# Self-attention with one score product: the maximum is subtracted by VectorE and the probabilities are transposed

## The reference

```python
scores = jnp.einsum('bhqd,bhkd->bhqk', q, k) * scale          # scale = 1/4
scores = jnp.where(causal[None, None], -jnp.inf, scores)      # mla and attn only
attn = jax.nn.softmax(scores, axis=-1)
out = jnp.einsum('bhqk,bhkd->bhqd', attn, v)
```

## Time and profile before

| what | value |
|---|---|
| median of 3 runs | 1013.06 us (1012.3 to 1020.51) |
| the profiled execution | 1020.58 us |
| its span, first to last instruction | 1018.5 us |
| PE, DVE, ACT busy | 971.9, 608.3, 450.8 us |
| TensorE clock granted, mean | 0.973 of full speed |

### The profile page before, as it was taken

One profiled execution on the slowest core, in us unless ns is written; L12 is line 12 of the kernel. 1 busy time (PEld: TensorE's weight loads), 2 busy tenths in 40 slices (PEclk: granted clock), 3 DMA queues, 4 the chain that ended last, 5 costly groups with the idle time before them and its releaser, 6 DMA issues.

```text
span 1018.5 us, 25940 instructions
## 1 busy us (share of the span) xinstructions
PE 971.9 (95%) x10769; PEld 832.1 (82%) x10769; DVE 608.3 (60%) x1427; ACT 450.8 (44%) x899; POOL 167.5 (16%) x357
## 2 busy tenths in 40 slices
PE   5999999999999989999879999997999999999998
PEld 5888888888888877788659999995888887877887
DVE  5745644554332646577579787777777763464242
ACT  3333333333333356655216666661444534574241
POOL 2312212113112113233330000003211200111000
PEclk9999999999999979999779999998999999999999
DMA  9400000000000092000028999964231002000000
GB/s 319 137 10 22 1 23 21 1 2 1 2 1 1 20 362 113 2 13 13 22 63 270 363 364 358 357 178 88 43 55 33 13 3 70 6 3 1 1 21 22
DMA packets 93763, 86.46 MB, mean 85 GB/s; under 512 B 42632, under 2 KB 85072, under 8 KB 93136
## 3 DMA queue, kind: packets, MB, share of 16 engines
q1 hardware_dynamic: 92112, 80.62, 24.8%
q0 software_dynamic: 1536, 4.20, 1.3%
HBM read 75.62 MB, written 9.18 MB: 83 GB/s over the span
## 4 chain that ended last, share of the span: by engine, by line
PE 86%; DVE 7%; ACT 4%; issue 2%; DMA 0%; POOL 0%; DVEq 0%; ACTq 0%; POOLq 0%
PE ps L632 9%; PE ps L647 9%; PE ps L2327 7%; PE ps L2340 6%; PE ps L2663 6%; PE ps L616 3%; PE ps L664 3%; PE ps L1446 3%; PE ps L1155 3%; PE ps L586 3%; PE ps L1543 3%; PE ps L684 3%; PE ps L1485 2%; PE ps L1080 2%; PE ps L1090 2%; PE ps L1527 2%
## 5 line engine op out<-in xcount | busy, mean ns | idle before, releaser
L2327 PE MATMUL ps<-moe_xT,ew 128*128 128x128 f32 x736 | 92.1, 280 | 2.2 <-issue 1.3
L775 ACT ACTIVATE x0pT<-ps 128x512 f32<-128x512 f32 x64 | 38.3, 598 | 123.6 <-PE ps L647 123.6
L2327 PEld LDWEIGHTS ps<-moe_xT,ew 128*128 128x128 f32 x736 | 88.4, 196 | 3.3 <-DVE moe_xT L2413 1.9
L385 POOL TENSOR_TENSOR rn_tmp<-rn_cur,eps 128x1 f32<-128x1 f32 x48 | 13.1, 273 | 354.0 <-DVE rn_cur L379 353.8
L890 DVE TENSOR_TENSOR x0A_lo<-ps,x0A_hi 128x512 fp32r<-128x512 f32 x64 | 41.1, 685 | 31.8 <-ACT x0A_hi L766 31.7
L2663 PE MATMUL ps<-f,ffw 128*128 128x512 f32 x256 | 59.1, 391 | 0.8 <-issue 0.6
L2663 PEld LDWEIGHTS ps<-f,ffw 128*128 128x128 f32 x256 | 47.7, 188 | 11.5 <-issue 0.9
L2340 PE MATMUL ps<-ew_2hi,eh_hi 128*128 128x256 f32 x184 | 55.4, 301 | 0.9 <-DVE eh_lo L2466 0.5
L2276 DVE TENSOR_TENSOR ew_2lo<-ew,ew_2hi 128x1024 fp32r<-128x1024 f32 x46 | 55.9, 1216 | 0.0
L2523 POOL DMA_INDIRECT yg<-moe_out,slot x16 | 16.1, 1006 | 232.3 <-DMA moe_out<-moe_y 163.5
L632 PE MATMUL ps<-x0wv_hi,x0cT_hi 128*128 128x512 f32 x128 | 52.8, 413 | 0.6 <-DVE x0A_lo L890 0.6
(11 more groups left out here) (332 smaller groups left out, 2459.9 us busy)
## 6 DMA issues: line engine op xcount, KB each, us to landing
ew<-L_ffn_W_dram SPq DMA_DIRECT2D x46, 1024.0 KB, 7.7
x0cin<-ctx_dram SPq DMA_DIRECT2D x8, 512.0 KB, 3.9
x1cin<-ctx_dram SPq DMA_DIRECT2D x64, 64.0 KB, 2.3
moe_out<-moe_y SPq DMA_DIRECT2D x23, 128.0 KB, 4.1
xg<-moe_in SPq DMA_DIRECT2D x21, 128.0 KB, 7.7
moe_in<-padneg SPq DMA_DIRECT2D x2, 1024.0 KB, 12.6
maskrow<-mask_BxS_ik_dram SPq DMA_DIRECT2D x2, 1024.0 KB, 7.6
x0wk<-L_xattn_Wkv_dram SPq DMA_DIRECT2D x1, 1024.0 KB, 7.1
```

The source lines that it names most:

```text
L775: nc.scalar.activation(g.pT[:, u, :], ps[:, S_BANK[u % 2], :], ACT.Exp, scale=64.0 ** -0.5).then_inc(C0.exp, 1)
L2327: last = nc.tensor.matmul(ps[:, n % 3, j * BT:j * BT + BT], ew1[b % NW][:, i, f * P:f * P + P], xT[b % 2][:, i, :], start=(i == 0), stop=( ...
```

## The change

The second score product goes away, with the negative maxima, their transposition, their tables and copies. After the maximum, DVE subtracts it from the scores in PSUM and writes the difference (128x1024, float32) to SBUF, into one of two tiles `sa_P` that lie in the memory of `xw`. ACT takes the exponential in place, one iteration earlier than before (item n+1 in iteration n). PE transposes the probabilities, eight 128x128 tiles in two ring fills "P0" and "P1" after `fill_pv` of n-1; ACT empties the first into the lower half of `sa_pT` (`pT_lower`), DVE the second into the upper half (`pT_upper`). The copy of k moves from DVE to ACT, that of v from ACT to DVE. The router's product comes after `fill_v`, and `fill_T` before it. Since `sa_P` uses its memory, `xw` is loaded later, at block 9 of the experts, with its axes exchanged. `keep_clock` issues 3, 4 and 3 matmuls where it issued 3, 2 and 2, and 2. The list `_more` says which fills DVE empties.

The diff, cut to its core:

```diff
+        sa_P = [nc.alloc_sbuf_tensor_at(f"sa_P{i}", [P, 4, D], F32, offset=xw_at + 16 * D * i) for i in range(2)]
...
-                FILLS += _routed(_n - 3, "router") + _at(_n + 2, "v") + _at(_n + 3, "hT") * _early + _at(_n - 1, "T", "y")
+                FILLS += _at(_n, "P0", "P1") + _at(_n - 1, "T") + _at(_n + 2, "v") + _routed(_n - 3, "router") + _at(_n + 3, "hT") * _early + _at(_n - 1, "y")
...
-        _more = [(n, "v") for n, (k, _) in enumerate(ITEMS) if k == "mla"] + [(n, k) for n, k in FILLS if k[0] == "A"]
+        _more = [(n, k) for n in range(3 * T) for k in ("v", "P1")] + [(n, k) for n, k in FILLS if k[0] == "A"]
...
             def scores(n):
...
-                if n > lo + 1:
-                    pe.wait_ge(SA.exp, n - 1)
-                elif n > lo:
-                    pe.wait_ge(SA.max, n)
+                if n > lo:
+                    pe.wait_ge(SA.shift, n)
...
-            def fill_neg(n):
...
-            def exponents(n):
...
+            def fill_P(n, half):
+
+                if half == 0:
+                    pe.wait_ge(SA.exp, n + 1)
+                RS.wait_free(pe, n, f"P{half}")
+                for i in range(4):
+                    r, hf = 2 * half + i // 2, i % 2
+                    last = nc.tensor.transpose(RS.bank(n, f"P{half}")[:, i * P:i * P + P], sa_P[n % 2][:, r, hf * P:hf * P + P], ident)
+                last.then_inc(SA.fill, 1)
 
             def fill_pv(n):
 
-                pe.wait_ge(SA.exp, n + 1)
+                RS.wait_emptied(pe, n, "P0")
+                RS.wait_emptied(pe, n, "P1")
...
             def exps(n):
-                act.wait_ge(SA.e_ps, n + 1)
-                nc.scalar.activation(g.pT[:, :, :], QS[:, :, 0:D], ACT.Exp, scale=0.25).then_inc(SA.exp, 1)
+                act.wait_ge(SA.shift, n + 1)
+                nc.scalar.activation(sa_P[n % 2][:, :, :], sa_P[n % 2][:, :, :], ACT.Exp, scale=0.25).then_inc(SA.exp, 1)
...
+                exps(lo)
...
             for n in range(lo, hi + (2, 1)[span]):
...
-                if here:
-                    exps(n)
+                if ahead:
+                    exps(n + 1)
...
             def maximum(n):
...
-                nc.vector.tensor_scalar(g.neg[:, :, 0:4], g.max[:, :, :], -1.0, None, ALU.mult).then_inc(SA.neg_hi, 1)
-                dve.wait_ge(SA.neg_hi, n + 1)
-                nc.vector.scalar_tensor_tensor(g.neg[:, :, 4:8], g.max[:, :, :], -1.0, g.neg[:, :, 0:4], ALU.mult, ALU.subtract).then_inc(SA.neg, 1)
...
+                nc.vector.tensor_tensor(sa_P[n % 2][:, :, :].rearrange("p r (f k) -> p r f k", f=4), QS[:, :, 0:D].rearrange("p r (f k) -> p r f k", f=4),
+                                        g.max[:, :, :].rearrange("p r (f o) -> p r f o", o=1).broadcast_to((P, 4, 4, N)), ALU.subtract).then_inc(SA.shift, 1)
...
-                elif front and (span == 0 or n > lo):
-                    k(n + 2)
                 if back:
                     attend(n - 1)
+                if here:
+                    pT_upper(n)
...
+                if front:
+                    v(n + 2)
...
-            for i, w in enumerate(("Wq", "Wk", "Wv", "Wo")):
-                whole(xw[:, :, i, :], weight("L1_xattn_" + w), ld["xw"])
...
+                if b == 9:
+                    RS.wait_filled(sp, 2 * T - 1, "P1")
+                    for i, w in enumerate(("Wq", "Wk", "Wv", "Wo")):
+                        whole(xw[:, i, :, :], weight("L1_xattn_" + w), ld["xw"])
```

More of the change, by code:

```diff
@@ L836, in self_tables @@
             dve.wait_ge(SA.tri, 1)
[L837 to L843, removed]
+            nc.vector.tensor_scalar(bqc_par[:, :], par_of, vec("bqc"), None, ALU.mult).then_inc(SA.tables, 2)
         def dve_x0(dve):
@@ L1171, in fill_y @@
                 for k in range(KD):
-                    last = nc.tensor.matmul(R1.bank(t, "y")[:, 0:D], g.attT[:, k, :], xw[:, k, 3, :], start=(k == 0), stop=(k == KD - 1))
+                    last = nc.tensor.matmul(R1.bank(t, "y")[:, 0:D], g.attT[:, k, :], xw[:, 3, k, :], start=(k == 0), stop=(k == KD - 1))
                 last.then_inc(C1.fill, 1)
@@ L1487, in scores @@
                 last.then_inc(SA.s_ps, 1)
-            def fill_neg(n):
-                pe.wait_ge(SA.neg, n + 1)
-                RS.wait_free(pe, n, "neg")
-                nc.tensor.transpose(RS.bank(n, "neg")[:, 0:N].bitcast(BF16), g.neg[:, :, :].rearrange("p r c -> p (r c)"), identb[:, :]).then_inc(SA.fill, 1)
-            def exponents(n):
[L1496 to L1512, removed]
-                                                    g.qbd[n % 3][32 * r:32 * r + 32, hf, b, :, :].rearrange("p a n -> p (a n)"),
-                                                    start=False, stop=True, skip_group_check=True)
-                last.then_inc(SA.e_ps, 1)
+            def fill_P(n, half):
[6 more added lines that the diff above has]
+                last.then_inc(SA.fill, 1)
             def fill_pv(n):
-                pe.wait_ge(SA.exp, n + 1)
+                RS.wait_emptied(pe, n, "P0")
+                RS.wait_emptied(pe, n, "P1")
                 pe.wait_ge(SA.v_frame, 3 * span + 3)
@@ L1692, in pe_self @@
                         fill_qk(n + 2, "q")
-                    if span == 0 and hi - 2 <= n <= hi:
-                        RS.wait_free(pe, n - 1, "T")
-                        keep_clock(RS.bank(n - 1, "T"), 3 if n == hi - 2 else 2)
                     if back:
@@ L1698, in pe_self @@
                 final = n - hi if span == 0 else None
-                if routed(span, n - 3):
-                    fill_router(n - 3)
+                if here:
+                    fill_P(n, 0)
+                    fill_P(n, 1)
                 if final == 1:
@@ L1704, in pe_self @@
                     place(5)
+                if final in (-2, -1, 0):
+                    RS.wait_free(pe, n - 1, "T")
+                    keep_clock(RS.bank(n - 1, "T"), 4 if final == -1 else 3)
+                if back:
+                    fill_T(n - 1)
                 if front:
                     fill_v(n + 2)
+                if routed(span, n - 3):
+                    fill_router(n - 3)
                 early = mla_pair(n + 2)
@@ L1824, in act_self @@
                 hT(lo)
+                k(lo)
                 x1_neg(t, 0)
@@ L1831, in act_self @@
                 x1_exps(t, 0)
+                k(lo + 1)
                 q(lo + 1)
-                v(lo + 1)
                 hT(lo + 2)
                 x1_exps(t, 1)
+                k(lo + 2)
                 x1_attT(t)
                 q(lo + 2)
+                exps(lo)
             for n in range(lo, hi + (2, 1)[span]):
-                here, front, back = lo <= n < hi, n + 2 < hi, lo <= n - 1 < hi
-                if here:
-                    neg(n)
+                here, ahead, front, back = lo <= n < hi, n + 1 < hi, n + 2 < hi, lo <= n - 1 < hi
                 if span == 1 and n > hi - 3:
                     f = 3 * (n - hi + 2)
-                    for i in range(f, min(f + 3, FT)):
-                        ff_relu(act, i)
-                if span == 1 and n == hi:
-                    ff_upper(act, 4)
-                    ff_upper(act, 5)
+                    ff_relu(act, f)
+                    if here:
+                        ff_relu(act, f + 1)
                 if is_mla(n + 2):
@@ L1880, in self_begin @@
         def self_begin(dve, span):
-            nc.vector.memset(SB.neg[:, :, :], 0.0).then_inc(SA.ready, 1)
+            dve.sem_inc(SA.ready, 1)
             if span == 1:
@@ L1988, in dve_self @@
             for n in range(lo, hi + (4, 1)[span]):
-                ahead, front, back = lo <= n + 1 < hi, n + 2 < hi, lo <= n - 1 < hi
+                here, ahead, front, back = lo <= n < hi, lo <= n + 1 < hi, n + 2 < hi, lo <= n - 1 < hi
                 if span == 1 and n == hi - 3:
```

141 lines of the change are left out of this document (72 added, 69 removed).

## The result

The changed kernel takes 1050.62 us (median of 4, 1047.35 to 1052.48) against 1016.78 for the kernel before in the same runs: a ratio of 1.0328, 95% interval 1.0261 to 1.0395. The forecast was 1035 against 1013.06, a ratio of 1.022. The direction and the mechanism came out. The size fell short: 33.8 us were lost and 22 forecast.

What follows compares the result with a forecast made beforehand. PE was taken as full, with DVE's queue setting when hT starts. Terms 7.0 + 2.0 + 3.3 + 2.6 - 2.0 + 1.0 = 13.9, with the clock 22, put on 1013.06: 1035 us; range 1006 to 1056, the forecast's own 1025 to 1047.

Steps and rivals of the forecast that it cites:

- Slot iterations: Iterations 9, 11, 13: hT starts 7.1 us after s, the start of probabilities times values; 2.35 lost each, +7.0 us.
- Iterations 10 and 12: Same walk with the shorter group for the top experts in place of the slots; 1.0 each, +2.0 us.
- Iterations 4, 6 and 8: An mla item is projected: transposed output 1.1 us later, the output projection waits for it; +3.3 us.
- Start: Iterations 0 to 3: ACT's queue carries two more table loads of 1.28 us each; +2.6 us.
- The clock: PE's waits in iterations 9, 11, 13 bring two or three further clock falls; +8 us, from 0 to 25.
- Experts and second cross-attention: Expert stage: 1 MB of weights loaded there is hidden behind expert weights; 2.9 us if that cover is gone.
- Iterations 5, 7 and the drain: Iterations 5 and 7, 14, 15 and the drain: late v costs 1.0 us in all, 0 to 2.
- The rival that PE's relief is kept: Late v and routing hidden, 17 us off, less table loads 14: 999; decided by h ready by about s+3.8; chance 0.12.
- span 1: Only 0.2 of PE's 0.86 us relief left, five times; first and last items another 1: -2.0, between 0 and -6.9.
- rule on weight loads: Weight loads, 6.91 of 8.89 us, would leave TensorE a fifth to spare: span 1's gain 0, sum 2 higher; not adopted.

Runs made afterwards that it cites:

- first experiment: Changed kernel with VectorE's normalized rows put directly behind the division, ahead of the copies of P1 and v and of routing: 1026.58 us.
- second: Changed kernel with the two copies back on their old engines in span 0, v on ScalarE and k on VectorE: 1042.7 us.
- The run with busy waits: Changed kernel with matmuls whose results nobody reads where PE waits, in iterations 0 to 2, 4, 6 and 8 to 12 of span 0: 1041.9 us.
- only ScalarE's order exchanged: Changed kernel with P0's copy, transposed output and early hT ahead of the rotated parts' gelu and table load, where an mla item is projected: 1033.92 us.
- the tail kept busy: Kernel with VectorE's and ScalarE's orders both exchanged, plus more matmuls whose results nobody reads in iterations 11, 12 and 14 to 16 of span 0: 1013.14 us.
- both orders: Changed kernel with VectorE's normalized rows behind the division and ScalarE's copy of P0, transposed output and early hT moved ahead: 1012.85 us, again 1012.25.

## Why the prediction was right, and where it was short

- *Slot iterations, "+7.0".* The walk was right to a tenth: hT at s+7.05 for 7.1. The measured 11.6 holds the clock's share too, which the forecast booked apart: iterations 9 and 11 ran at 0.75 and 0.86. Iteration 13, at full clock before and after, lost 2.27 for the 2.35 taken. It has no hT, which the walk overlooked; there the transposes of u, in the same place of DVE's queue, wait 2.61. Moving the normalized rows (first experiment) and moving v's copy (second) show that it is this queue.
- *Iterations 10 and 12, "+2.0".* Measured 4.8. Iteration 10 ran partly at the lower clock, 0.76 in the mean. At full clock iteration 12 lost 1.3, near the 1.0 taken.
- *Iterations 4, 6 and 8, "+3.3".* Measured 6.0: 0.9, 2.4 and 2.7. Iteration 4 is near the 1.1 of the walk; in 6 the clock fell, and in 8 hT also waited 1.05 for h and the router's product 1.52 for P0's copy, which the walk had not followed. That ACT's queue is the cause in 4 and 6 is shown by exchanging its order: each then takes 9.31, against 9.57 and 9.34 before; iteration 8 still takes 10.54.
- *Start, "+2.6".* Measured 4.0. The term was named wrongly: "two more table loads" are not the cost; with both loads in place and the copies ahead of them iteration 0 is shorter than before, at the same clock.
- *The clock, "+8, from 0 to 25".* This term was the most undersized. The run with busy waits gave back 9, but its matmuls ran over by 7.6, so the clock's share up to iteration 14 is nearer 15 by the estimate above, and at the entry of span 1 it cost 3.4 more (below). Two or three further falls were expected, and five came, some of them in iterations that the forecast had not named (3 and 6). The 9 beside the 8 is therefore luck. That PE's waits bring the falls of span 0 is shown, since filling them keeps the clock at 1.00.
- *Experts and second cross-attention, 0.* Measured +2.7. Where the cross-attention begins the granted clock is low for some 14 us (728 to 742), against some 10 before (703 to 713). That differs from run to run: with the tail kept busy the same stretch took 323.9, less than before. Whether the later load of `xw` has a part in it was not tried alone.
- *Iterations 5, 7 and the drain, "1.0".* Measured -1.2, at a low clock on both sides in the drain, so this says little of the schedule.
- *The rival that PE's relief is kept* was right about the size of the relief and wrong about the queue. Its condition, h ready at s+3.8, is what the first experiment makes true, and then an iteration takes 7.6. Its time of 999 was not reached by any version: with both orders iterations 10 and 12 together still take 3.8 us more than before.

The step whose mechanism failed is *span 1, "-2.0"*: it measured +3.6. The steady items gain 0.27 each, for 0.2 forecast, and the last items 1.05, for 1; the entry lost 5.5, and I had not walked through it. Two things add up there. PE in the first iteration of span 1, after: v, then hT.

```profile
891.66 1.03 PE L1447 MATMUL ps<-w_sq,sa_hT 128*128 128x256 f32 x4
895.39 0.53 PE L1406 MATMUL ps<-cst,h 128*128 128x128 f32 x2 [2.70 <-DVE h L405]
```

hT waits 2.70 us for h, again behind DVE's copies. From the first to the third score product of span 1 it is 13.0 us, against 9.9 before; with VectorE's order exchanged, and nothing else, it is 9.1. The second thing is the clock. Windows from the first score product of span 1 to the second, of the changed kernel and of the one with only ScalarE's order exchanged:

```profile
883.69:889.67 5.98, 5.98 (x51) 5.31 (x50) 2.77 (x3) 2.25 (x5) 0.00 (x0) 0.58 0.00 0
862.00:866.27 4.27, 3.88 (x51) 3.11 (x50) 3.31 (x5) 2.03 (x5) 0.00 (x0) 1.00 0.02 4
```

In the changed kernel the clock was already low here, from 882 us on, although PE had been busy without a gap for the 40 us before. ScalarE's order (mla items only) changes nothing in span 1, and neither does the exchange of the two copies; in both traces the clock is full at this place, hT still waits, and span 1 takes 77.3 us, 0.2 more than before, not 3.6. The trace with busy waits has the fall and takes 80.7. So the wait at the entry, with the clock that falls behind it, used up the gain of 2.0; the other 3.4 come with a fall of the clock that had begun before span 1, and its cause stays open.

The Trainium skill's rule on weight loads as the measure of TensorE ("Perfetto Trace Analysis", Identifying the Most-Contended Engine), as the prediction reads it, would have made removed PE work worth little. With the waits gone the items of span 1 became 1.02 us shorter, all that PE was relieved of and a little more; so here, where groups stand close behind each other, the matmul rows were the better guide.

## What to carry to other kernels

When work moves to an engine that has time in the sum, look at where it goes in that engine's queue, and at what the bound engine takes from the end of it: the same instructions cost 24 us ahead of the normalized rows, the clock included, that they did not cost behind them. Put first what the bound engine waits for, and only then weigh totals. Count a new wait of TensorE for itself and again for the clock that it may bring down; here the second was about as large as the first, by the estimate above. And check that work added to fill a wait is no longer than the wait: what such a run gives back is otherwise too small.

## What the runs showed of the hardware

With PE's waits filled, the granted clock over 148 us rose from 0.88 to 1.00 and 9 of 1050 us went, although the filling ran over by 7.6. The clock also fell where PE had not waited: at 882 us of the changed kernel, after 40 us without a gap. Eight float32 transposes of 128x128 came out at 0.12 us each although each is listed with 286 ns. The subtraction of a broadcast operand from PSUM into SBUF took the 1.22 us of a plain maximum over the same columns.
